# One decoder block on one core: residual loads per group, fills moved at the begin, and the last norm of self attention handed to cross attention's first batches

## Chip, cores, metric

One core of one Trainium2 chip. The metric is the device time of one execution in microseconds; the program is one launch. The matrices are f32; where a product needs more speed than f32 has, a value is kept as a high and a low part of type fp32r.

## The reference, cut

64 batches of 128 tokens with 128 features. All three parts end in a residual sum and a layer norm without weights.

```python
x = _layernorm(x + _L0_attn_ref(x, W_qkv, b_qkv, W_proj, b_proj))
x = _layernorm(x + _L0_xattn_ref(x, ctx_768, mask, Wq, Wk, Wv, Wo))
x = _layernorm(x + _L0_ffn_ref(x, phi_w, phi_b, expert_w, expert_b))
...
def _L0_attn_ref(...):
    attn = jnp.einsum('bsd,btd->bst', q, k) * SCALE
    attn = jax.nn.softmax(sps_pro(attn), axis=-1)   # x * mult, mult from four thresholds of sigmoid(x)
    return jnp.einsum('bst,btd->bsd', attn, v) @ W_proj + b_proj
def _L0_xattn_ref(...):                             # 16 heads of 8, 77 keys of 96 features
    scores = jnp.einsum('bhid,bhjd->bhij', q, k) * scale
    attn = jax.nn.softmax(jnp.where(mask, scores, -max), axis=-1)
    return jnp.einsum('bhij,bhjd->bhid', attn, v) @ Wo
```

The third part (soft mixture of 64 experts with 32 slots) is not touched by the change.

## The kernel before

The program is a row of blocks. In a block each engine has its own list, written out by hand; engines meet at semaphores (`wait_ge`; `reach` is the same but skips a wait for zero or less). A block ends when all five engines, SP with its DMA issues among them, have come to its end; only then does the next begin.

**`setup`** (L78 to L153). SP loads the weights and constants, ACT's queue the weights of cross attention. DVE spreads two biases (`brep`, L122), PE folds the weights of self attention (L145 to L153), DVE copies the results (L128 to L133). POOL fills partitions 96 to 127 of `w.xh` with ones (L138); `xh` and `xl` are the high and low part of the transposed x for the third part, whose row 127 is a constant row.

**`attention`** (L156 to L409). 16 groups of 4 batches; step k works on several groups at once. Group g passes through `groups(k, lag)`: products and scores at lag 0; thresholds (`band`, L352 to L357 on DVE, sums of them on POOL, L222 and L225), maxima and exponentials at lag 1; turning the weights and multiplying with the values at lag 2 (psum tile `O`); residual, statistics on DVE (L378 to L394) and the root on POOL (L228, L231) at lag 3; scaling on ACT (L309) and turning on PE (L296) at lag 4; the copy to `x1T` (L318) at lag 5. The steps run to GROUPS + 5. POOL first issues four loads of 1 MB of residuals into `xres`, fills `xl` (L214) and the two `pack` tiles (L217, L218). SP loads xT group by group (L237), two ahead. Near the end, steps 16 and 17 also make queries and keys of the first two pairs of batches for cross attention: PE L267 and L268, ACT's high part (L339), DVE's low part (L409). SP stores each pair to DRAM and loads it back in another layout:

```python
for r in FIRST:
    sync.wait_ge(w.low_ready, r + 1)
    store_and_pack(sync, w, r)
```

`store_and_pack` (L411) issues one store of the halves, waits for it, waits until the pack tile is free (`t_made`, counted in batches), and issues six loads into it.

**`attend_context`** (L428 on). Batch n = 0 to 63, pair r = n // 2. POOL multiplies packed keys (L822), PE makes scores in two halves (L567), DVE their maxima (L730), PE turns the maxima (L541) and makes turned scores and their shift (L579, L587, which raises `t_made`), ACT takes exponentials (L661), and one or more batches later PE, DVE and ACT do values, residual and norm. PE, ACT and DVE also make queries, keys (L528, L529) and values (L534) of later pairs. POOL clears two tiles (L813) and DVE three `vd` tiles in the first steps.

Of the kernel before, what the change touches and what calls it, by code (L numbers as in the profile page):

```python
# [18 lines left out]
ALU = mybir.AluOpType  # L19
ACT = mybir.ActivationFunctionType  # L20
X = mybir.AxisListType.X
F32 = mybir.dt.float32
# [55 lines left out]
def setup(nc, io, w):  # L78

    with ExitStack() as ctx:  # L80
# [54 lines left out]
        @block.gpsimd  # L135
        def _(pool):

            pool.memset(w.xh[96:128].bitcast(F32), 1.0)  # L138
# [16 lines left out]

def attention(nc, io, w):  # L156
# [3 lines left out]
    x_in = io["x"].rearrange("(q b s) d -> q s b d", q=4, s=S)  # L160
    with ExitStack() as ctx:
        st = Store(nc, ctx, "attn")
        xTg = [st.sb(f"xTg{i}", [128, GB * 128]) for i in range(2)]
# [9 lines left out]
        sums = [st.sb(f"sums{i}", [128, GB]) for i in range(2)]  # L173
        pT = [st.sb(f"pT{i}", [128, 512]) for i in range(2)]
        rinv = st.sb("rinv", [128, GB])
        y = [st.sb(f"y{i}", [128, GB, 128]) for i in range(2)]
        stats = st.sb("stats", [128, GB, 6])
        mv = [st.sb(f"mv{i}", [128, GB, 2]) for i in range(2)]
        veps = st.sb("veps", [128, GB])
        rstd = [st.sb(f"rstd{i}", [128, GB]) for i in range(2)]  # L180
        shift = [st.sb(f"shift{i}", [128, GB]) for i in range(2)]
        psU, psS, psT, psX = (st.ps(n, [128, 512]) for n in ("U", "S", "T", "X"))
        psO = [st.ps(f"O{i}", [128, 512]) for i in range(2)]
        psV = st.ps("V", [128, 2, 512])
        V = psV[:, :, 0:258].rearrange("p i (b e) -> p i b e", b=2)

        xT_loaded = [st.sem("xT_loaded0"), st.sem("xT_loaded1")]
        x_loaded = [st.sem(f"x_loaded{q}") for q in range(4)]
        (u_made, v_made, s_made, uT_ready, v_ready, rb_ready, a_ready, f_ready, p_ready, pT_made, pT_ready,
         o_made, mv_ready, rstd_ready, shift_ready, x1_ready, x1T_made, x1T_kept, low_ready, mult_ready, band_done, top_done,  # L190
         mx_done, y_chain, pool_chain) = (
            st.sem(n) for n in ("u_made", "v_made", "s_made", "uT_ready", "v_ready", "rb_ready", "a_ready",
                                "f_ready", "p_ready", "pT_made", "pT_ready", "o_made", "mv_ready",
                                "rstd_ready", "shift_ready", "x1_ready", "x1T_made", "x1T_kept", "low_ready",
                                "mult_ready", "band_done", "top_done", "mx_done", "y_chain", "pool_chain"))
        fill_made, row_set = st.sem("fill_made"), st.sem("row_set")
        WIDE = 256 + 2 * JP
        FIRST = range(2)
# [8 lines left out]
        STEPS = range(GROUPS + 5)  # L207

        @block.gpsimd
        def _(pool):  # L210
            for q in range(4):
                pool.dma_start(w.xres[:, q * 2048:(q + 1) * 2048].rearrange("s (b d) -> s b d", d=D), x_in[q])\
                    .then_inc(x_loaded[q], 16)
            pool.memset(w.xl[96:128].bitcast(F32), 0.0).then_inc(row_set, 1)  # L214
            pool.wait_ge(row_set, 1)
            for i in range(2):
                pool.tensor_copy(w.pack[i][:, :, 0:256], w.fill_row.unsqueeze(2).to_broadcast([128, 4, 256]))  # L217
                pool.memset(w.pack[i][:, :, 256:WIDE].bitcast(F32), 0.0).then_inc(w.pack_set, 1)  # L218
            for k in STEPS:
                for g in groups(k, 1):  # L220
                    pool.wait_ge(band_done, 2 * g + 2)
                    pool.tensor_tensor(band[4][:], band[1][:], band[2][:], ALU.add).then_inc(low_ready, 1)  # L222
                    pool.wait_ge(low_ready, g + 1)
                    reach(pool, f_ready, g)
                    pool.tensor_tensor(band[5][:], band[4][:], band[3][:], ALU.add).then_inc(mult_ready, 1)  # L225
                for g in groups(k, 3):
                    pool.wait_ge(mv_ready, g + 1)
                    pool.tensor_tensor(veps[:], mv[g % 2][:, :, 1], w.eps[:, 0:GB], ALU.add).then_inc(pool_chain, 1)  # L228
                    pool.wait_ge(pool_chain, g + 1)
                    reach(pool, x1_ready, g - 1)  # L230
                    pool.tensor_tensor(rstd[g % 2][:], veps[:], w.neg_half[:, 0:GB], ALU.pow).then_inc(rstd_ready, 1)  # L231

        @block.sync
        def _(sync):
            for g in range(GROUPS):
                reach(sync, s_made, g - 1)
                sync.dma_start(xTg[g % 2][:], io["xT"][:, residual(g)]).then_inc(xT_loaded[g % 2], 16)  # L237
                if g == 1:
                    sync.wait_ge(fill_made, 1)
                    sync.dma_start(w.fill_by_batch, w.fills[:]).then_inc(w.fill_stored, 16)  # L240
            for r in range(3):
                sync.dma_start(w.cg[r][:], io["ctxT"][:, r * 2 * JP:(r + 1) * 2 * JP]).then_inc(w.c_loaded[r], 16)
            sync.wait_ge(w.pack_set, 2)
# [6 lines left out]
        def _(pe):  # L250
            for k in STEPS:
# [10 lines left out]
                for r in [k - GROUPS] if k - GROUPS in FIRST else []:  # L262
                    pe.wait_ge(x1T_kept, 1)
                    pe.wait_ge(uT_ready, GROUPS)
                    reach(pe, w.low_ready, r)
                    pe.wait_ge(w.c_loaded[r], 16)
                    pe.matmul(psU[:, 0:256], w.xqs[:], w.x1T[:, r * 256:(r + 1) * 256], start=True, stop=True)  # L267
                    pe.matmul(psU[:, 256:WIDE], w.xk[:], w.cg[r][:], start=True, stop=True).then_inc(w.qk_made, 1)  # L268
                for g in groups(k, 2):
# [5 lines left out]
                    ins.then_inc(pT_made, 1)  # L275
                for g in groups(k, 0):
# [14 lines left out]
                for g in groups(k, 4):  # L291
                    pe.wait_ge(x1_ready, g + 1)
                    reach(pe, x1T_kept, g)
                    for b in range(GB):
                        c = slice(b * 128, (b + 1) * 128)
                        ins = pe.transpose(psX[:, c], w.xres[:, residual(g)][:, c], w.ident)  # L296
                    ins.then_inc(x1T_made, 1)

        @block.scalar
        def _(act):  # L300
            for k in STEPS:
# [4 lines left out]
                for g in groups(k, 4):  # L306
                    act.wait_ge(shift_ready, g + 1)
                    for b in range(GB):
                        ins = act.activation(w.xres[:, residual(g)][:, b * 128:(b + 1) * 128], y[g % 2][:, b, :],  # L309
                                             ACT.Identity, bias=shift[g % 2][:, b:b + 1], scale=rstd[g % 2][:, b:b + 1])  # L310
                    ins.then_inc(x1_ready, 1)
                for g in groups(k, 2):
                    act.wait_ge(pT_made, g + 1)
                    reach(act, o_made, g - 1)
                    act.copy(pT[g % 2][:], psT[:]).then_inc(pT_ready, 1)
                for g in groups(k, 5):
                    act.wait_ge(x1T_made, g + 1)
                    act.copy(w.x1T[:, residual(g)], psX[:]).then_inc(x1T_kept, 1)  # L318
                for g in groups(k, 0):
# [6 lines left out]
                    ins.then_inc(a_ready, 1)  # L326
                for g in groups(k, 1):
# [8 lines left out]
                for r in [k - GROUPS] if k - GROUPS in FIRST else []:  # L336
                    act.wait_ge(w.qk_made, r + 1)
                    reach(act, w.stored, 16 * r)
                    act.copy(w.qk[:, 0, :], psU[:, 0:WIDE]).then_inc(w.high_ready, 1)  # L339

        @block.vector
        def _(dve):
# [4 lines left out]
            for k in STEPS:  # L347
# [10 lines left out]
                for g in groups(k, 4):  # L358
                    dve.wait_ge(rstd_ready, g + 1)
                    reach(dve, x1_ready, g - 1)  # L360
                    dve.scalar_tensor_tensor(out=shift[g % 2][:], in0=mv[g % 2][:, :, 0], scalar=-1.0,
                                             in1=rstd[g % 2][:], op0=ALU.mult, op1=ALU.mult).then_inc(shift_ready, 1)
# [9 lines left out]
                for g in groups(k, 3):  # L372
                    if g == 0:
                        for q in range(4):
                            dve.wait_ge(x_loaded[q], 16)
                    dve.wait_ge(p_ready, g + 1)
                    reach(dve, mv_ready, g)
                    dve.reciprocal(rinv[:], sums[g % 2][:]).then_inc(y_chain, 1)  # L378
                    dve.wait_ge(o_made, g + 1)
                    dve.wait_ge(y_chain, 3 * g + 1)  # L380
                    reach(dve, x1_ready, g - 1)
                    for b in range(GB):
                        c = slice(b * 128, (b + 1) * 128)
                        ins = dve.scalar_tensor_tensor(out=y[g % 2][:, b, :], in0=psO[g % 2][:, c], scalar=rinv[:, b:b + 1],
# [1113 lines left out]
```

## Time and profile before

| | us |
|---|---|
| median of 3 runs | 1399.61 |
| all runs | 1399.61, 1403.23, 1399.18 |
| the profiled execution, its time | 1401.92 |
| its span | 1399.9 |

Busy over the span: PE 1293.0 us (92%), DVE 1109.3 (79%), ACT 896.6 (64%), POOL 1180.2 (84%). The mean granted TensorE clock is 0.975 of full speed. The profile was taken of one execution. Its rows have a start or a stretch in microseconds from the span's begin; "idle before" is time in which the engine did nothing before the row, with the event that ended it. An average over the span mixes stages with different limits, so the stretches around the change are read by themselves.

### The profile page before, as it was taken

How to read it: one execution, taken by the hardware profiler on the slowest of the kernel's cores; microseconds unless marked ns; L12 is line 12 of the kernel's file. 1: busy time of each engine (PE TensorE's matmuls, PEld its weight loads, DVE VectorE, ACT ScalarE, POOL GpSimd, SP SyncE). 2: the span in 40 equal slices, each digit the busy share in tenths (PEclk: the TensorE clock that was granted, in tenths of full speed). 3: DMA queues.
4: the chain of work that ended last, by engine and by line, in shares of the span. 5: the costliest groups of instructions: out<-in, count | busy, mean ns of one | idle time of the engine just before them, and what ended most of it. 6: DMA issues, size and time to landing. Idle time of an engine off the chain costs nothing. (4 is left out here: it accounts for less than half of the span.)

```text
span 1399.9 us, 31677 instructions
## 1 busy us (share of the span) xinstructions
PE 1293.0 (92%) x11006; PEld 1055.0 (75%) x11006; DVE 1109.3 (79%) x2462; ACT 896.6 (64%) x1670; POOL 1180.2 (84%) x1050
## 2 busy tenths in 40 slices
PE   4886789999999699999999999979999999999998
PEld 3664567777676477777777777748999999999997
DVE  4897456666666688888888888877999999999996
ACT  2897356666666476776776777735666666666664
POOL 7664568888888399999999999967999999999997
PEclk9998699999999999999999999999999999999999
DMA  5111243443443022222222222212222223232321
GB/s 167 47 40 55 84 134 117 121 122 115 125 121 94 24 84 89 92 83 91 91 84 90 91 87 87 84 48 94 84 88 83 88 84 89 82 91 80 92 79 31
DMA packets 83567, 123.61 MB, mean 88 GB/s; under 512 B 8593, under 2 KB 54226, under 8 KB 83410
## 3 DMA queue, kind: packets, MB, share of 16 engines
q1 hardware_dynamic: 81810, 117.16, 26.4%
q0 software_dynamic: 1088, 4.19, 1.0%
q8 instruction: 90, 1.47, 0.4%
q14 instruction: 67, 0.55, 0.1%
q10 hardware_dynamic: 512, 0.23, 0.1%
HBM read 70.28 MB, written 51.27 MB: 87 GB/s over the span
## 5 line engine op out<-in xcount | busy, mean ns | idle before, releaser
L997 POOL TENSOR_TENSOR gather_d<-gather_e,gather_rinv 128x1024 f32<-128x1024 f32 x128 | 244.8, 1913 | 36.6 <-DVE gather_rinv L976 36.5
L1256 POOL TENSOR_TENSOR mix_c<-mix_e,mix_rinv 128x1024 f32<-128x1024 f32 x128 | 240.9, 1902 | 18.7 <-DVE mix_rinv L1244 16.6
L1324 PEld LDWEIGHTS last_Y<-kept_phi,last_cT 128*128 128x128 f32 x2048 | 248.4, 192 | 7.3
L1324 PE MATMUL last_Y<-kept_phi,last_cT 128*128 128x128 f32 x2048 | 249.0, 275 | 0.0
L1340 ACT COPY last_cT<-last_T 128x1024 f32<-128x1024 f32 x128 | 128.4, 1003 | 132.1 <-PE last_T L1331 132.1
L822 POOL TENSOR_TENSOR cross_kd<-first_pack,kept_consts 128x624 fp32r<-128x624 f32 x128 | 155.6, 1237 | 63.7 <-DMA first_pack<-first_halves 54.1
L730 DVE TENSOR_REDUCE cross_mx<-cross_S 128x8 fp32r<-128x624 f32 x128 | 103.5, 809 | 113.0 <-PE cross_S L567 113.0
L1241 DVE TENSOR_REDUCE mix_sums<-mix_e 128x16 f32<-128x1024 f32 x128 | 155.8, 1217 | 34.4 <-ACT mix_e L1215 34.0
L972 DVE TENSOR_REDUCE gather_rsum<-gather_e 128x32 f32<-128x1024 f32 x128 | 156.1, 1220 | 25.9 <-ACT gather_e L945 25.9
L991 POOL TENSOR_TENSOR gather_dl<-gather_d,gather_dh 128x512 fp32r<-128x512 f32 x128 | 166.5, 1301 | 0.0
L934 ACT COPY gather_keep<-gather_L 128x256 f32<-128x256 f32 x256 | 94.7, 370 | 96.2 <-PE gather_L L908 95.9
L1331 PE MATMUL last_T<-kept_consts,mix_c 128*128 128x128 f32 x1024 | 134.2, 274 | 3.2 <-POOL mix_c L1256 1.1
L945 ACT ACTIVATE gather_e<-gather_L 128x1024 f32<-128x1024 f32 x128 | 131.1, 1024 | 7.5
L661 ACT ACTIVATE cross_pT<-cross_P 77x1024 f32<-77x1024 f32 x128 | 131.2, 1028 | 2.1 <-PE cross_P L587 2.1
L922 PE MATMUL slots_X<-gather_d,kept_xres 128*128 128x512 f32 x256 | 130.7, 592 | 0.0
L1249 POOL TENSOR_TENSOR mix_less<-mix_read,mix_high 128x1024 f32<-128x1024 f32 x64 | 122.5, 1914 | 7.4 <-DVE mix_high L1231 4.3
L1331 PEld LDWEIGHTS last_T<-kept_consts,mix_c 128*128 128x128 f32 x1024 | 114.6, 142 | 4.5 <-issue 2.5
L966 DVE TENSOR_REDUCE gather_mx<-gather_L 128x16 fp32r<-128x512 f32 x128 | 88.5, 691 | 30.3 <-PE gather_L L908 21.4
L927 PE MATMUL slots_X<-gather_dh,gather_x2h 128*128 128x512 f32 x128 | 101.0, 789 | 3.0 <-POOL gather_dl L991 3.0
L957 ACT CAST gather_dh<-gather_d 128x512 fp32r<-128x512 f32 x128 | 79.5, 621 | 31.6 <-PE slots_X L929 19.7
L968 DVE TENSOR_REDUCE gather_mx<-gather_L 128x16 fp32r<-128x512 f32 x128 | 87.0, 680 | 0.0
L908 PE MATMUL gather_L<-over_w1h,kept_xh 128*128 128x512 f32 x256 | 81.5, 400 | 4.3 <-ACT gather_e L945 3.3
(205 smaller groups left out, 3013.0 us busy)
## 6 DMA issues: line engine op xcount, KB each, us to landing
kept_logits<-gather_keep SPq DMA_DIRECT2D x128, 256.0 KB, 2.0
mix_read<-kept_logits SPq DMA_DIRECT2D x64, 512.0 KB, 3.7
first_halves<-first_qk SPq DMA_DIRECT2D x32, 412.0 KB, 3.0
first_pack<-first_halves SPq DMA_DIRECT2D x64, 128.0 KB
first_pack<-first_halves SPq DMA_DIRECT2D x32, 206.0 KB
first_pack<-first_halves SPq DMA_DIRECT2D x64, 78.0 KB
attn_xTg<-in_xT SPq DMA_DIRECT2D x16, 256.0 KB, 2.6
kept_xres<-in_x POOLq DMA_DIRECT2D x4, 1024.0 KB, 12.1
```

What stands on the lines that cost most here:

```text
L661: act.activation(pT[n % 2][0:J, hs, :, :], psP[:, hs, :, :], ACT.Exp)\
L822: pool.tensor_tensor(kd[n % 2][:, q], keys[:, q].to_broadcast([128, 2, 4, JP]), w.own.unsqueeze(1).unsqueeze(3).to_broadcast([128, 2, 4, J ...
L922: pe.matmul(psX[:, 2 * j + 1, :], w.xres[:, rows(u)], dd[u % 4][:, 1, :], start=first, stop=last)\
L945: act.activation(e[u % 2][:], psL[u % 2][:].rearrange("p i (n s) -> p i n s", n=16), ACT.Exp)\
L972: dve.tensor_reduce(rsum[u % 2][:].rearrange("p (i n) -> p i n", i=2), e[u % 2][:], X, ALU.add)\
L991: pool.tensor_tensor(dl[u % 2][:], dd[u % 4][:, 0, :], dh[u % 2][:], ALU.subtract).then_inc(dl_ready, 1)
L997: pool.tensor_tensor(dd[u % 4][:].rearrange("p i (n s) -> p i n s", n=16), e[u % 2][:], rinv[u % 2][:].rearrange("p (i n) -> p i n", i=2). ...
L1241: dve.tensor_reduce(self.sums[u % 2][:], self.e[u % 2][:], X, ALU.add).then_inc(self.sum_done, 1)
L1256: pool.tensor_tensor(self.cc[u % 2][:], self.e[u % 2][:], self.rinv[u % 2][:].unsqueeze(2).to_broadcast([128, 16, EXPERTS]), ALU.mult)\
L1324: ins = pe.matmul(psY[t % 2][:, 0:128], cT[u % 2][:, c, :], w.yk[:, 8 * (u % 2) + c, :], start=(u % 2 == 0 and c == 0), stop=(u % 2 == 1 a ...
L1331: ins = pe.transpose(psT[:, c, :], mix.cc[u % 2][:, 2 * c:2 * c + 2, :], w.ident)
L1340: act.copy(cT[u % 2][:], psT[:]).then_inc(cT_ready, 1)
```

## The change

- `setup`: SP also loads xT of groups 0 and 1, into tiles that now live outside `attention`. POOL's fill of `xh` goes; POOL fills the two pack tiles there, after `brep` (`rep` 3).
- `attention`: SP loads the residuals of each group behind that group's xT, 256 KB each; DVE waits for its group's. The constant rows of `xh` and `xl` come from a DRAM input by DMA, one partition each. The fills of `xl` and of the pack tiles and POOL's loads go. The steps run to GROUPS + 3. Pair 0's high part on ACT stands ahead of the last exponentials (L421 in the new order below), pair 1's queries and keys behind the last turning of weights.
- The norm of self attention becomes a class, `FirstNorm`, whose parts both blocks call. Group 14 is scaled and turned in cross attention, group 15 also summed, with statistics, root and shift there. They are turned in the psum tile `O` of cross attention, which lies on the bank of `O` of group 15.
- `attend_context`: SP begins with pair 1's store and packing. PE makes the first half of batch 0's scores first, then turns group 14, makes pair 2's queries and keys, and own values of pair 0 after the turned scores. The constant tile `pick`, which was made first, comes after batch 0's maxima.

```diff
@@ setup
+            for g in range(2):
+                sync.dma_start(w.xTg[g][:], io["xT"][:, g * 512:(g + 1) * 512]).then_inc(w.xT_loaded[g], 16)
             sync.dma_start(w.mask[:], io["mask"]).then_inc(w.mask_loaded, 16)
...
-            pool.memset(w.xh[96:128].bitcast(F32), 1.0)
+            pool.wait_ge(rep, 3)
+            for i in range(2):
+                pool.tensor_copy(w.pack[i][:, :, 0:256], w.fill_row.unsqueeze(2).to_broadcast([128, 4, 256]))
+                pool.memset(w.pack[i][:, :, 256:256 + 2 * JP].bitcast(F32), 0.0)
@@ attention
-        STEPS = range(GROUPS + 5)
+        def but_last(k, lag, left):
+            return [k - lag] if 0 <= k - lag < GROUPS - left else []
+        STEPS = range(GROUPS + 3)
...
-            for q in range(4):
-                pool.dma_start(w.xres[:, q * 2048:(q + 1) * 2048].rearrange("s (b d) -> s b d", d=D), x_in[q])\
-                    .then_inc(x_loaded[q], 16)
-            pool.memset(w.xl[96:128].bitcast(F32), 0.0).then_inc(row_set, 1)
...
-                reach(sync, s_made, g - 1)
-                sync.dma_start(xTg[g % 2][:], io["xT"][:, residual(g)]).then_inc(xT_loaded[g % 2], 16)
+                if g >= 2:
+                    sync.wait_ge(s_made, g - 1)
+                    sync.dma_start(xTg[g % 2][:], io["xT"][:, residual(g)]).then_inc(xT_loaded[g % 2], 16)
+                reach(sync, x_loaded[g % 4], 16 * (g // 4))
+                sync.dma_start(w.xres[:, residual(g)].rearrange("s (b d) -> s b d", d=D), x_in[g])\
+                    .then_inc(x_loaded[g % 4], 16)
...
+                if g == 3:
+                    sync.wait_ge(row_set, 16)
+                    sync.dma_start(w.xh[127:128].bitcast(F32), w.rows[0:1]).then_inc(row_set, 16)
+                    sync.dma_start(w.xl[127:128].bitcast(F32), w.rows[1:2]).then_inc(row_set, 16)
...
-            for r in FIRST:
-                sync.wait_ge(w.low_ready, r + 1)
-                store_and_pack(sync, w, r)
+            sync.wait_ge(w.low_ready, 1)
+            store_and_pack(sync, w, 0)
...
+                for g in but_last(k, 3, 1):
+                    dve.wait_ge(x_loaded[g % 4], 16 * (g // 4 + 1))
+                    norm.add_residual(dve, g, psO[g % 2])
@@ attend_context, SP
+            sync.wait_ge(low_ready, 2)
+            store_and_pack(sync, w, 1)
@@ attend_context, PE
                 if is_batch(n):
                     scores(n, 0)
+                if n == 0:
+                    pe.wait_ge(norm.y_chain, 3 * LAST + 2)
+                    norm.turn(pe, LAST - 1, all_O)
+                    queries_keys(2)
+                if n == 2:
+                    pe.wait_ge(norm.x1T_kept, LAST + 1)
...
+                if n == 1:
+                    norm.turn(pe, LAST, all_O)
@@ attend_context, ACT
+            norm.normalise(act, LAST - 1)
             for n in STEPS:
...
+                if n == 0:
+                    norm.keep_turned(act, LAST - 1, all_O)
...
+                if n == 0:
+                    keep_values(0)
+                    norm.normalise(act, LAST)
+                if n == 1:
+                    norm.keep_turned(act, LAST, all_O)
@@ attend_context, DVE
+            norm.add_residual(dve, LAST, w.last_O)
+            clear_values(0)
...
+                if n == 0:
+                    dve.tensor_copy(pick[:], w.sel.unsqueeze(2).to_broadcast([128, 4, JP])).then_inc(pick_set, 1)
+                    norm.find_shift(dve, LAST)
+                    clear_values(1)
@@ attend_context, POOL, between the keys of batch 0 and 1
+                if n == -1:
+                    norm.invert_spread(pool, LAST)
+                    pool.wait_ge(norm.rstd_ready, LAST + 1)
```

`FirstNorm`'s parts are the statements of before (L378 to L394, L228 to L231, L361, L309, L296, L318) with the group as argument.

How the rows move: SP's queue at the seam between the two attentions. Before, from the last context loads to the first load of cross attention (`first_halves` is the DRAM copy, `first_pack` the packed tile):

```order
L242 DMA first_cg<-in_ctxT 96x156 x3
L415 DMA first_halves<-first_qk 128x2x412
L420 DMA first_pack<-kept_fill 4x4x156
L424 DMA first_pack<-first_halves 32x1648
...
L415 DMA first_halves<-first_qk 128x2x412
L420 DMA first_pack<-kept_fill 4x4x156
L424 DMA first_pack<-first_halves 32x1648
...
L161 UNCONDITIONAL_BRANCH
L500 UNCONDITIONAL_BRANCH
L505 DMA first_cg<-in_ctxT 96x156
```

And now:

```order
L323 DMA first_cg<-in_ctxT 96x156 x3
L480 DMA first_halves<-first_qk 128x2x412
L485 DMA first_pack<-kept_fill 4x4x156
L489 DMA first_pack<-first_halves 32x1648
...
L248 UNCONDITIONAL_BRANCH
L568 UNCONDITIONAL_BRANCH
L480 DMA first_halves<-first_qk 128x2x412
L485 DMA first_pack<-kept_fill 4x4x156
L489 DMA first_pack<-first_halves 32x1648
...
L573 DMA first_cg<-in_ctxT 96x156
```

The block's end (the branches) stands before pair 1's store now, and the load of context 3 behind pair 1's packing.

PE at the same seam, from the last values of self attention. Before (`attn_X` are turned groups, `cross_M` queries, keys or values, `cross_S` scores, `cross_P` turned scores and shift):

```order
L289 MATMUL attn_O1<-attn_vp0,attn_pT1 128x128 x4
L296 MATMUL attn_X<-kept_consts,kept_xres 128x128 x12
L161 UNCONDITIONAL_BRANCH
L516 UNCONDITIONAL_BRANCH
L534 MATMUL cross_M<-first_xv,first_cg0 77x128 x2
L528 MATMUL cross_M<-first_x1T,first_xqs 128x256
L529 MATMUL cross_M<-first_cg2,first_xk 128x156
L567 MATMUL cross_S<-cross_kd0,first_pack0 128x312 x4
L541 MATMUL cross_M<-kept_neg_ident,cross_mx0 128x128
L579 MATMUL cross_P<-first_pack0 77x128 x16
L587 MATMUL cross_P<-cross_mT,cross_pick 77x128 x16
```

Now:

```order
L374 MATMUL attn_O1<-attn_vp0,attn_pT1 128x128 x4
L235 MATMUL attn_X<-kept_consts,kept_xres 128x128 x4
L248 UNCONDITIONAL_BRANCH
L586 UNCONDITIONAL_BRANCH
L637 MATMUL cross_S<-cross_kd0,first_pack0 128x312 x2
L235 MATMUL cross_O<-kept_consts,kept_xres 128x128 x4
L598 MATMUL cross_M<-first_x1T,first_xqs 128x256
L599 MATMUL cross_M<-first_cg2,first_xk 128x156
L637 MATMUL cross_S<-cross_kd0,first_pack0 128x312 x2
L611 MATMUL cross_M<-kept_neg_ident,cross_mx0 128x128
L649 MATMUL cross_P<-first_pack0 77x128 x16
L604 MATMUL cross_M<-first_xv,first_cg0 77x128 x2
```

Two turns of four have left the old block; the first scores stand first, one turn between their halves, and the own values of pair 0 behind the turned scores.

## Rows read from the trace of the kernel before

**Rows 1.** Windows: start:end, length, busy (count) by engine, PEclk, DMA share, GB/s

```profile
40.00:60.00 20.00, 15.65 (x110) 12.81 (x109) 18.67 (x94) 15.88 (x54) 13.40 (x13) 1.00 0.14 40
140.00:160.00 20.00, 11.56 (x91) 8.89 (x92) 7.42 (x14) 4.70 (x8) 13.39 (x10) 0.50 0.18 56
240.00:250.00 10.00, 9.36 (x160) 7.02 (x160) 6.59 (x21) 6.59 (x15) 8.41 (x11) 1.00 0.39 117
```

The busy columns are PE, PEld, DVE, ACT and POOL.

**Rows 2.** Order of time, POOL, the begin: start, duration, engine, line, what

```profile
0.72 6.92 POOL L138 MEMSET kept_xh<- 32x8192 f32 x1 [0.29 <-POOLq L1488]
...
18.13 6.95 POOL L214 MEMSET kept_xl<- 32x8192 f32 x1
...
28.99 1.26 POOL L222 TENSOR_TENSOR attn_band<-attn_band 128x512 f32<-128x512 f32 x1
```

**Rows 3.** Order of time, DVE, the begin

```profile
5.13 2.66 DVE L122 TENSOR_SCALAR setup_brep<-setup_ones,setup_bqkv 128x128 f32<-128x128 f32 x2 [4.10 <-DMA kept_consts<-in_consts]
...
21.05 4.32 DVE L352 TENSOR_SCALAR attn_band<-attn_a 128x512 f32<-128x512 f32 x1 [1.31 <-ACT attn_a L325]
...
32.68 0.43 DVE L352 TENSOR_SCALAR attn_band<-attn_a 128x512 f32<-128x512 f32 x1
...
38.16 0.43 DVE L352 TENSOR_SCALAR attn_band<-attn_a 128x512 f32<-128x512 f32 x1
```

**Rows 4.** Order of time, PE, the begin

```profile
7.94 0.77 PE L145 MATMUL setup_pa<-setup_wT 128*128 128x128 f32 x2 [7.94 <-DVE setup_brep L122]
...
15.36 2.08 PE L255 MATMUL attn_U<-attn_xTg,first_m 128*128 128x512 f32 x2 [3.80 <-DMA attn_xTg<-in_xT]
```

**Rows 5.** Order of time, SP's queue, the begin

```profile
12.76 0.81 SPq L237 DMA_DIRECT2D attn_xTg<-in_xT  x2
```

**Rows 6.** Order of time, SP's queue, the seam

```profile
126.80 0.39 SPq L415 DMA_DIRECT2D first_halves<-first_qk  x1
129.47 0.61 SPq L420 DMA_DIRECT2D first_pack<-kept_fill  x1
130.13 3.19 SPq L424 DMA_DIRECT2D first_pack<-first_halves  x5
133.37 0.59 SPq L415 DMA_DIRECT2D first_halves<-first_qk  x1
138.41 0.55 SPq L420 DMA_DIRECT2D first_pack<-kept_fill  x1
138.99 3.06 SPq L424 DMA_DIRECT2D first_pack<-first_halves  x5
```

**Rows 7.** Order of time, ACT and POOL, the seam

```profile
124.05 0.40 ACT L333 ACTIVATE attn_pr<-attn_f,attn_nb 128x128 f32<-128x128 f32 x1 [1.21 <-DVE attn_nb L406]
...
125.61 0.48 ACT L339 CAST first_qk<-attn_U 128x412 fp32r<-128x412 f32 x1
...
142.73 2.50 POOL L822 TENSOR_TENSOR cross_kd<-first_pack,kept_consts 128x624 fp32r<-128x624 f32 x2 [7.31 <-POOLq L161]
```

**Rows 8.** Order of time, all engines: the last group's norm

```profile
131.61 1.13 DVE L384 SCALAR_TENSOR_TENSOR attn_y<-attn_O,attn_rinv,kept_xres 128x128 f32<-128x128 f32 x4 [0.50 <-PE attn_O L289]
...
134.42 1.01 POOL L231 TENSOR_TENSOR attn_rstd<-attn_veps,kept_neg_half 128x4 f32<-128x4 f32 x1
...
135.66 1.65 ACT L309 ACTIVATE kept_xres<-attn_y,attn_shift,attn_rstd 128x128 f32<-128x128 f32 x4 [2.48 <-DVE attn_shift L361]
```

**Rows 9.** Order of time, PE: one turn, and the shift of batch 1

```profile
131.37 1.06 PE L296 MATMUL attn_X<-kept_consts,kept_xres 128*128 128x128 f32 x4
...
157.80 0.73 PE L587 MATMUL cross_P<-cross_mT,cross_pick 32*77 32x128 f32 x16
```

**Rows 10.** Order of time, ACT and PE, batches 6 to 8

```profile
183.44 0.50 ACT L683 CAST first_qk<-cross_M 128x412 fp32r<-128x412 f32 x1 [3.02 <-DMA first_halves<-first_qk]
...
186.37 0.76 PE L587 MATMUL cross_P<-cross_mT,cross_pick 32*77 32x128 f32 x16
...
193.30 0.47 PE L587 MATMUL cross_P<-cross_mT,cross_pick 32*77 32x128 f32 x16
...
198.22 0.47 PE L587 MATMUL cross_P<-cross_mT,cross_pick 32*77 32x128 f32 x16
```

More of the change, by code:

```diff
@@ L225, in _ @@
                     pool.tensor_tensor(band[5][:], band[4][:], band[3][:], ALU.add).then_inc(mult_ready, 1)
[L226 to L231, printed above, removed]
+                for g in but_last(k, 3, 1):
+                    norm.invert_spread(pool, g)
         @block.sync
@@ L261, in _ @@
                     ins.then_inc(v_made, 1)
[L262 to L268, printed above, removed]
+                if k == GROUPS:
+                    queries_keys(0)
                 for g in groups(k, 2):
@@ L290, in _, with keep_weights, high_part @@
                     ins.then_inc(o_made, 1)
[L291 to L297, printed above, removed]
+                for g in but_last(k, 4, 2):
+                    norm.turn(pe, g, psX)
         @block.scalar
         def _(act):
+            def keep_weights(k):
+                for g in groups(k, 2):
+                    act.wait_ge(pT_made, g + 1)
+                    reach(act, o_made, g - 1)
+                    act.copy(pT[g % 2][:], psT[:]).then_inc(pT_ready, 1)
+            def high_part(r):
+                act.wait_ge(w.qk_made, r + 1)
+                reach(act, w.stored, 16 * r)
+                act.copy(w.qk[:, 0, :], psU[:, 0:WIDE]).then_inc(w.high_ready, 1)
             for k in STEPS:
@@ L305, in _ @@
                     act.activation(uT[:], psU[:], ACT.Identity, bias=w.cvec[:]).then_inc(uT_ready, 1)
[L306 to L318, printed above, removed]
+                if k >= GROUPS:
+                    keep_weights(k)
+                for g in but_last(k, 4, 2):
+                    norm.normalise(act, g)
+                if k < GROUPS:
+                    keep_weights(k)
+                for g in but_last(k, 5, 2):
+                    norm.keep_turned(act, g, psX[:])
                 for g in groups(k, 0):
@@ L335, in _ @@
                     ins.then_inc(p_ready, 1)
[L336 to L339, printed above, removed]
+                if k == GROUPS + 1:
+                    high_part(1)
         @block.vector
@@ L357, in _ @@
                     dve.tensor_scalar(band[2][:], av, T_01, -0.4, ALU.is_lt, ALU.mult).then_inc(band_done, 1)
[L358 to L362, printed above, removed]
+                for g in but_last(k, 4, 1):
+                    norm.find_shift(dve, g)
+                if k == STEPS[-1]:
+                    for q in range(4):
+                        dve.wait_ge(x_loaded[q], 64)
                 for g in groups(k, 0):
@@ L371, in _ @@
                        .then_inc(v_ready, 1)
[L372 to L384, printed above, removed]
[L385 to L395 removed]
+                for g in but_last(k, 3, 1):
+                    dve.wait_ge(x_loaded[g % 4], 16 * (g // 4 + 1))
+                    norm.add_residual(dve, g, psO[g % 2])
                 for g in groups(k, 1):
@@ L1437, in decoder_block @@
             w.halves = nc.dram_tensor("first_halves", (2, 2, 128, wide), F32, kind="Internal").ap()
-            w.qk_made, w.high_ready, w.low_ready, w.stored, w.pack_set, w.t_made = (
-                sf.sem(n) for n in ("qk_made", "high_ready", "low_ready", "stored", "pack_set", "t_made"))
+            w.qk_made, w.high_ready, w.low_ready, w.stored, w.t_made = (
+                sf.sem(n) for n in ("qk_made", "high_ready", "low_ready", "stored", "t_made"))
             w.packed = [sf.sem("packed0"), sf.sem("packed1")]
-            setup(nc, io, w)
-            attention(nc, io, w)
+            w.norm = FirstNorm(sf, w)
+            with ExitStack() as early:
+                w.xTg = [early.enter_context(nc.sbuf_tensor(f"first_xTg{i}", [128, 512], F32)) for i in range(2)]
+                setup(nc, io, w)
+                attention(nc, io, w)
             x1T_space.close()
@@ L1485 @@
         "expert_w": get("L0_ffn_expert_w"), "expert_bT": get("L0_ffn_expert_b").T,
-        "consts": constants(),
+        "consts": constants(), "rows": np.stack([np.ones(TOKENS, np.float32), np.zeros(TOKENS, np.float32)]),
     }
```

182 lines of the change are left out of this document (127 added, 55 removed).

## Prediction

> **What bounds the kernel now.** I read the windows by stage first, to find which engine is full where; then the order of time on POOL, DVE and PE over the first 45 us; then the order of time around the seam between the two attentions, on SP's queue above all. Everything behind the first batches of cross attention is left alone by the change.
>
> In self attention DVE is the full engine: 18.67 of 20 us from 40 to 60 [rows 1], and one group of four batches costs DVE some 6 us. In cross attention PE is full: 9.36 of 10 us in a late window [rows 1]. From 140 to 160 nobody is: PE 11.56, DVE 7.42 of 20 us, with PE's granted clock at 0.50, the 1.2 GHz level [rows 1]. So there are two places with time to give, the begin and the seam, and each is a chain of waits, not a sum of work.
>
> The begin. POOL fills a quarter of `xh` until 7.64 (0.72 + 6.92) and a quarter of `xl` until 25.08 (18.13 + 6.95) [rows 2]. Two small DVE instructions behind the first fill show 2.66 us and end at 7.79; one DVE comparison that takes 0.43 elsewhere shows 4.32 and ends at 25.37, right behind the second fill [rows 2, 3]. PE starts its folding at 7.94, 0.15 us after the first of these ends, is done at 11.56 (15.36 less 3.80), and waits those 3.80 for a load of xT that SP issued at 12.76, with the start of the block [rows 4, 5]. POOL reaches its first addition of `band` at 28.99 [rows 2], so the first comparison of the second group comes 11.63 us after that of the first (21.05 to 32.68); the next follows in 5.48 [rows 3].
>
> The seam. SP stores pair 0's halves at 126.80, waits 2.67, issues six packing loads in 3.85, stores pair 1 at 133.37, waits 5.04 and issues six more, until 142.05 (138.99 + 3.06) [rows 6]. Only then does the block end: POOL's first key product starts at 142.73, released by the block's branch and not by its data [rows 7].
>
> **The change, part by part.** Sums are against the profiled execution: 1401.92 us, a span of 1399.9. The median of the runs is 1399.61, 2.3 below, and I take the same gain off it.
>
> 1. *No fill of xh.* DVE's two products start at 5.13; alone they are an estimate of 0.1 to 0.2 us each (0.43 for four times the columns [rows 3]), so they end at 5.5 instead of 7.79. The PE folding hangs on them directly: **-2.3**. Cost of what moves in: the two pack fills, 3.9 us in all on POOL (25.08 to 28.99 [rows 2]), run from 5.5 to 9.4 now. PE's folding ends at 9.2 (11.56 less 2.3), DVE's copies come behind it, and the block starts at 10.5 (12.76 less 2.3), so POOL is covered. If DVE's three small instructions in between wait for all of POOL's, DVE reaches its copies at 10.0 rather than 9.25: the bounds are 0 and +0.8. I take 0, since the copies wait for PE anyway.
> By the Trainium skill (SBUF — State Buffer, "Who interferes with whom") whichever of DVE in a two-port mode and GpSimd issues first holds the shared ports for its whole instruction, and the other fully blocks. The 4.32 us agree; by that rule the moved fills speak against this part, and the sum would be 0.8 us higher.
>
> 2. *xT loaded in setup.* Issued at 3.0 and landed long before 10. PE's first matmul starts with the block, 12.8 less 2.3, rather than at 15.36: **-2.6**. The two loads now stand ahead of the mask and behind the constants on SP; they can delay the constants, released at 5.13, by between nothing and about half a microsecond. I take nothing.
>
> 3. *No fill of xl, no pack fills and no four 1 MB loads at the head of POOL's list.* The first group's comparison takes 0.43, POOL adds right away, and the distance to the second group's becomes the 5.48 of the next pair in place of 11.63 [rows 3]: **-6.15**. The third xT load, in flight beside 4 MB of residuals before, is no longer late. What takes their place: one residual load of 256 KB per group on SP's queue, two issues per group instead of one where SP waits for PE most of the time. Each is issued two groups ahead of the DVE step that reads it, more than 12 us. Two rows of 32 KB go to one partition each; no row shows such a load, but nothing waits for them until the first packing, 100 us later. Cost nothing; one more DVE wait per group, fifteen times under 0.1 us.
>
> Begin: 2.3 + 2.6 + 6.15 = **-11.0**, and self attention, full on DVE, carries it to the seam unchanged.
>
> 4. *Pair 0's high part ahead of the last exponentials.* Times here are those of the trace before, without the 11.0. The exponentials take ACT from 124.05 to 125.61 [rows 7]; the copy now comes before them, where ACT had waited 1.21 for DVE, at about 123.8. DVE is done with the last maxima at 124.0 and makes the low part at once. The store moves from 126.80 to 125.0: **-1.8**. Its price, some 0.3 us of later exponentials, lies beside the store.
>
> 5. *Pair 1's store and packing behind the block's end, the last two groups' turn and the last group's norm too.* SP: store at 125.0, landed 127.7 (2.67), packing issued by 131.5 (3.85) [rows 6]. DVE and ACT end at about 130.9 by the same walk, two groups' chains shorter. So the block ends at 131.5 and the next begins at 132.2 (0.68 as before, 142.05 to 142.73). Now data bind: pair 0's packing lands later than the branch. No row shows when a packing lands. From both sides: a lone store of the same halves took 2.28 from the end of its issue (127.19 to 129.47), the store behind a packing 5.04 from its start [rows 6]; the least is the block's own 0.68. I take 2.3, since nothing stands ahead of this packing: the first key product comes at 133.8 instead of 142.73, **-8.9** with the 1.8 of point 4 in it; the bounds make it 10.5 to 6.2.
>
> 6. *What comes into the first batches.* One norm is a chain of 5.7 us, from DVE's first sum at 131.61 over POOL's root (134.42, 1.01) to the end of ACT's scaling at 137.31 [rows 8]. DVE's part of it, 2.8 us (131.61 to 134.42), comes ahead of its first maximum, from 132.3 to 135.1 with one clearing behind it, at 136; the first scores are not there before 135.9 (first half of the keys 1.25 after 133.8, then 0.9 of PE). POOL's root stands between the keys of batch 0 and 1 and is done before PE asks for the latter. PE has two turns more, 1.06 each at the low level [rows 9]; the first fills PE's wait for the first maximum, and the own values of pair 0 move behind it. Walking each queue: PE's shift of batch 1, which frees the pack for pair 2, ends 16.0 us after the first key product, and 15.8 before (142.73 to 158.53 [rows 7, 9]). Cost **+0.2**; bounds 0 and +3.0. Pair 1's packing: store at 132.3, 5.04, 3.85 of issues, 2.3 of landing, 143.5, about when POOL first asks for it and 6 us before PE needs its keys. Behind batch 1 the queues stand in the old order, and PE-bound cross attention carries the gain on.
>
> Sum: -11.0 - 8.9 + 0.2 = -19.7. Profiled 1382.2; **1379.9 us** on the median, a gain of 1.4%. A measurement of this kernel can tell about 0.3%, 4.2 us, from no change.
>
> **The rivals.**
> *The moved work lies on the path again (0.12).* The last norm's chain (5.7 us) and two turns (2.1 us) stand before batch 1's shift and come one behind another: 7.8 of the 8.9 go back, **1387.7**. For it: every engine has it early in its list, and in-order queues pass a wait on. Against it: PE was idle for 8.4 of 20 us in exactly that stretch [rows 1].
> *The old stall goes (0.07).* ACT waited 3.02 for a store of the halves, until 183.44, and the batch after took 6.93 (PE's shifts at 186.37 and 193.30) instead of 4.92 (to 198.22) [rows 10]. If the new spacing of SP's work misses it, 5 us more are gained: **1374.9**. Against it: that piece of SP's list is unchanged and hangs on PE's shifts.
> *The begin does not do what it says (0.04).* The pack fills were moved, not removed, and the early loads share the rings with the constants; point 1 and 2 lose most of their 4.9: **1384**.
> *Slower: PE stays at 1.2 GHz (0.04).* The seam's low stretch ends only when PE has become busy again. The new first batches have more short waits between PE's pieces. A batch at the low level costs 6.93 against 4.92 [rows 10], 2.0 more; the gain of 19.7 is gone after 10 batches more at that level, and "slower" is reached from 12. With 16, **1412**. For it: 0.50 held over all of 140 to 160 [rows 1]. Against it: with the same batch order PE got out of it before, while idle more than it will be. The Trainium skill (TensorE: Matmul & The Clock Gate, "The HAM clock gate") says that throttled is the default and activity releases it, which would favour this rival where idle gaps grow; here they shrink.
>
> **How the numbers follow.** The forecast has 0.73. Its own bounds (0.8, 0.5, 2.7 and 1.6 of landing, 3.0) give 1378 to 1387. To hold 8 in 10 I reach to the stall's case below and the path's case above: 1373 to 1389. Faster: all but the last rival, 0.96; half of that rival's 0.04 ends within 0.3%, half above: same 0.02, slower 0.02.
>
> **What would show it.** PE's folding starting near 5.6 and the first self attention matmul near 10.5 with no DMA wait; the comparisons of groups 0 and 1 5.5 apart, at 16.2 and 21.7; a DVE-full stretch with no wait for `in_x`; the first key product near 122.8 and released by DMA; PE's second shift ending near 138.8. Wrong would be: a first comparison of 4 us in spite of the missing fill, DVE waits for residual loads, PE at 1.2 GHz beyond 145, or a first maximum of batch 0 that starts on DVE's account and not PE's.

## The result, and the profile after

Median 1380.79 us (1379.94 to 1382.79, 4 runs) against 1399.39 (1397.85 to 1403.23, 4 runs) for the kernel before: a ratio of 0.9865, 95% interval 0.9846 to 0.9884, so 18.6 us less, between 16 and 22. The profiled execution took 1381.27 us, with a span of 1379.2.

The begin, in order of time, DVE and POOL of the changed kernel (start, duration, engine, line, what, idle time before and its releaser). They answer to [rows 2, 3].

```profile
5.67 0.48 DVE L124 TENSOR_SCALAR setup_brep<-setup_ones,setup_bqkv 128x128 f32<-128x128 f32 x2 [4.64 <-DMA kept_consts<-in_consts]
6.07 0.22 DVE L125 CAST kept_ident<-kept_consts 128x128 f16<-128x128 f32 x1
6.21 0.22 DVE L126 TENSOR_SCALAR kept_neg_ident<-kept_consts 128x128 fp32r<-128x128 f32 x1
6.34 1.06 DVE L128 TENSOR_SCALAR first_xqs<-first_xq 128x128 f32<-128x128 f32 x1
9.96 0.29 DVE L130 COPY first_m<-setup_pa 128x128 f32<-128x128 f32 x1 [2.56 <-PE setup_pb L158]
...
16.98 0.43 DVE L438 TENSOR_SCALAR attn_band<-attn_a 128x512 f32<-128x512 f32 x1 [1.31 <-ACT attn_a L411]
...
22.47 0.43 DVE L438 TENSOR_SCALAR attn_band<-attn_a 128x512 f32<-128x512 f32 x1
```

```profile
6.22 1.10 POOL L142 CAST first_pack<-kept_consts 128x1024 fp32r<-128x1024 f32 x1 [5.80 <-DVE setup_brep L124]
...
8.88 0.61 POOL L143 MEMSET first_pack<- 128x624 f32 x1
18.77 1.27 POOL L298 TENSOR_TENSOR attn_band<-attn_band 128x512 f32<-128x512 f32 x1 [9.27 <-DVE attn_band L443]
```

The two products take 0.48 and not 2.66, the first comparison 0.43 and not 4.32, and the second comes 5.49 behind the first and not 11.63. POOL is done with the pack fills at 9.49, before DVE's copies at 9.96, and then waits 9.27 for DVE. PE, to compare with [rows 4]:

```profile
6.30 0.77 PE L150 MATMUL setup_pa<-setup_wT 128*128 128x128 f32 x2 [6.30 <-DVE setup_brep L124]
...
11.16 2.04 PE L343 MATMUL attn_U<-first_xTg,first_m 128*128 128x512 f32 x2 [1.24 <-PEq L80]
```

The wait of 3.80 for xT is now one of 1.24 for the block's start. The seam on SP's queue and POOL, against [rows 6, 7]:

```profile
114.32 0.38 SPq L480 DMA_DIRECT2D first_halves<-first_qk  x1
117.31 0.62 SPq L485 DMA_DIRECT2D first_pack<-kept_fill  x1
117.98 3.08 SPq L489 DMA_DIRECT2D first_pack<-first_halves  x5
121.71 0.39 SPq L480 DMA_DIRECT2D first_halves<-first_qk  x1
124.58 0.57 SPq L485 DMA_DIRECT2D first_pack<-kept_fill  x1
125.19 3.06 SPq L489 DMA_DIRECT2D first_pack<-first_halves  x5
```

```profile
123.41 2.43 POOL L920 TENSOR_TENSOR cross_kd<-first_pack,kept_consts 128x624 fp32r<-128x624 f32 x2 [5.08 <-DMA first_pack<-first_halves]
```

The block ends behind pair 0's packing (121.06), and the first key product waits for data, no longer for the branch: it starts 2.35 after the last issue. PE's shift of batch 1, against [rows 9]:

```profile
132.00 0.78 PE L657 MATMUL cross_P<-cross_mT,cross_pick 32*77 32x128 f32 x16
138.10 0.73 PE L657 MATMUL cross_P<-cross_mT,cross_pick 32*77 32x128 f32 x16
```

It ends at 138.83, 15.42 after the first key product. One of the prediction's signs of being wrong stands on its edge: the first maximum of batch 0 shows no wait for PE. PE's first scores ended at 125.65 and DVE's clearing at 125.68:

```profile
124.79 0.86 PE L637 MATMUL cross_S<-cross_kd,first_pack 128*128 128x312 f32 x2 [5.34 <-POOL cross_kd L920]
125.59 0.09 DVE L808 MEMSET cross_vd<- 128x32 f32 x1
125.76 0.81 DVE L819 TENSOR_REDUCE cross_mx<-cross_S 128x8 fp32r<-128x624 f32 x1
```

In the trace with the early xT loads behind the constants (an experiment below) the scores ended at 125.23 and the maximum started at 125.57, so there it was on DVE's account, by some 0.3 us. And the old stall is still there, against [rows 10]:

```profile
164.24 0.50 ACT L771 CAST first_qk<-cross_M 128x412 fp32r<-128x412 f32 x1 [4.01 <-DMA first_halves<-first_qk]
```

The same points in the kernels before and after and in those of the first two experiments, read from the order of time in each:

| us from the span's begin | constants release DVE | second comparison | first key product | shift of batch 1 ends | wait of ACT at pair 5 | median time |
|---|---|---|---|---|---|---|
| before | 5.13 | 32.68 | 142.73 | 158.53 | 3.02 | 1399.39 |
| changed | 5.67 | 22.47 | 123.41 | 138.83 | 4.01 | 1380.79 |
| begin alone | 5.09 | 22.36 | 130.17 | 145.97 | 4.07 | 1388.99 |
| seam alone | 5.08 | 32.68 | 136.13 | 150.61 | 2.36 | 1390.85 |
| begin, store moved | 5.41 | 22.76 | 129.63 | 145.43 | 4.11 | 1388.30 |
| begin, norm moved | 5.00 | 22.73 | 129.52 | 145.13 | 4.08 | 1387.44 |

### The profile page after: what moved, and what is told of

The parts are those of the page before. It is cut to its first block and busy times, and to the rows that moved or that the text cites. A ratio compares the mean times of both kernels' runs of the same rounds, so it can differ in the third digit from the quotient of the medians.

```text
span 1379.2 us, 31693 instructions
## 1 busy us (share of the span) xinstructions
PE 1286.2 (93%) x11006; PEld 1050.8 (76%) x11006; DVE 1105.5 (80%) x2462; ACT 896.5 (65%) x1670; POOL 1162.0 (84%) x1044
## 5 line engine op out<-in xcount | busy, mean ns | idle before, releaser
L1067 DVE TENSOR_REDUCE gather_mx<-gather_L 128x16 fp32r<-128x512 f32 x128 | 88.6, 692 | 29.6 <-PE gather_L L1009 20.7
```

## The experiments

### Do the two parts add?

`begin alone` is the kernel before with the change's setup, loads and rows; the seam is left as it was.

```diff
+            for g in range(2):                       # setup, as in the change
+                sync.dma_start(w.xTg[g][:], io["xT"][:, g * 512:(g + 1) * 512]).then_inc(w.xT_loaded[g], 16)
...
             for r in FIRST:                          # attention, as before
                 sync.wait_ge(w.low_ready, r + 1)
                 store_and_pack(sync, w, r)
```

> The begin of the change alone (early xT, residual loads per group, constant rows by DMA, pack fills in setup); the seam is that of before. Theory A (two chains that add): the comparison of the last group comes about 10.3 us earlier (near 108.1, as in the changed kernel), the first key product near 132.4 (142.73 less 10.3), time near 1389. Theory B (the begin's gain is swallowed by a later wait or given back by the 16 more loads): the last comparison near 110 or later, time above 1393.

Measured: 1388.99 us (4 runs) beside 1398.20 (7 runs) of the kernel before, ratio 0.9926 (0.9908 to 0.9945). The last group's comparison stands at 107.99, 10.45 earlier. The first key product, though, is at 130.17, 12.6 earlier and not 10.3. The reason is in its SP queue, against the fourth and fifth of [rows 6]:

```profile
122.76 0.59 SPq L418 DMA_DIRECT2D first_halves<-first_qk  x1
125.84 0.56 SPq L423 DMA_DIRECT2D first_pack<-kept_fill  x1
```

Pair 1's store waits 3.08 here, 5.04 in the profile of the kernel before. The last experiment below, which has the old begin and the old seam, shows 3.05 and its key product at 140.75. From the last group's comparison to the first key product the profile of before has 24.29, `begin alone` 22.18 and that last experiment 22.21. So some 2 us of the old seam look like that one profiled execution's own, which was also 2.5 above the median; no second trace of the kernel before itself was taken.

`seam alone` is the changed kernel with the old setup, fills and four 1 MB loads:

```diff
-            pool.wait_ge(rep, 3)
-            for i in range(2):
-                pool.tensor_copy(w.pack[i]...)
+            pool.memset(w.xh[96:128].bitcast(F32), 1.0)
...
+            for q in range(4):
+                pool.dma_start(w.xres[:, q * 2048:(q + 1) * 2048]..., x_in[q]).then_inc(x_loaded[q], 16)
+            pool.memset(w.xl[96:128].bitcast(F32), 0.0).then_inc(row_set, 1)
```

> The seam of the change alone; setup, POOL's fills and its four 1 MB loads are those of before. Theory A (the two parts add): first comparison at 21.05 and 32.68 as before, first key product near 133.7 (142.73 less 9.0), shift of batch 1 ending near 149, time near 1390. Theory B (the seam depends on what the begin freed): key product later than 136, time above 1394.

Measured: 1390.85 us (4 runs), ratio 0.9941 (0.9921 to 0.9962). The second comparison is at 32.68, but the last group's at 121.12, 2.7 later than in the kernel before: DVE waited once for PE inside self attention, at 55.45, where the granted clock is 0.50 from 50 to 55 (0.83 over 40 to 60). Why it fell there was not tested.

```profile
DVE attn_rb L443 <- PE attn_V L341: 2.7, 1, 2.7
```

(Waits of DVE from 44 to 112: who waited for whom, us, times, longest.) From the last comparison to the key product it takes 15.01, in the changed kernel 15.32, with the begin alone 22.18. So the seam is worth 6.9 (22.18 less 15.32) with the new begin and 7.2 (22.21, from the last experiment, less 15.01) with the old, and theory A holds, with this size in place of 9.0. Its key product at 136.13 lies just past the 136 of theory B; the 2.7 are what carried it there. Saved by the begin 9.2, by the seam 7.4, by both 18.6, each with 2 to 3 us of uncertainty: they add within it.

### What of the seam carries it?

Once only the store and packing of pair 1 move, once only the norms. The first diff is to `begin alone`, the second to the changed kernel.

```diff
-            for r in FIRST:
-                sync.wait_ge(w.low_ready, r + 1)
-                store_and_pack(sync, w, r)
+            sync.wait_ge(w.low_ready, 1)
+            store_and_pack(sync, w, 0)
@@ attend_context
+            sync.wait_ge(low_ready, 2)
+            store_and_pack(sync, w, 1)
```

> The begin of the change, and of the seam only pair 1's store and packing moved behind the block's end; the last groups' norms stay in self attention. Theory A (SP and the norm chain end within 3 us of each other, so that both must move): the block ends with ACT's last copy, 139.62 less 10.3, key product near 130, time near 1386.6, only 2.4 below the begin alone. Theory B (SP's list alone held the block): key product near 125.2, time near 1382.

```diff
-            sync.wait_ge(w.low_ready, 1)
-            store_and_pack(sync, w, 0)
+            for r in range(2):
+                sync.wait_ge(w.low_ready, r + 1)
+                store_and_pack(sync, w, r)
@@ attend_context
-            sync.wait_ge(low_ready, 2)
-            store_and_pack(sync, w, 1)
```

> The changed kernel with pair 1's store and packing back in the self attention block. Theory A: SP stores pair 1 at 121.1, packs from 124 to 126 until 128 to 130, block end behind it, key product between 128.5 and 130.5, time near 1387. Theory B (the norm chain alone held the block): key product near 123.4, time near 1381.

Measured: 1388.30 and 1387.44 us (2 runs each), ratios 0.9924 (0.9901 to 0.9948) and 0.9918 (0.9890 to 0.9947). The first key product of each, in this order:

```profile
129.63 2.51 POOL L826 TENSOR_TENSOR cross_kd<-first_pack,kept_consts 128x624 fp32r<-128x624 f32 x2 [4.50 <-POOLq L166]
```

```profile
129.52 2.43 POOL L919 TENSOR_TENSOR cross_kd<-first_pack,kept_consts 128x624 fp32r<-128x624 f32 x2 [10.34 <-POOLq L248]
```

Both wait for the block's end, as before. Against the begin alone (130.17) each half gains under 1 us; with both moved it is 6.8. Counted from the last group's comparison it is 1.0, 1.6 and 6.9. What held the block is the norm chain's last copy on ACT in the first, until 129.34, and SP's packing in the second, until 128.85:

```profile
128.75 0.59 ACT L322 COPY first_x1T<-attn_X 128x512 f32<-128x512 f32 x1 [1.27 <-PE attn_X L300]
```

```profile
125.78 3.07 SPq L490 DMA_DIRECT2D first_pack<-first_halves  x5
```

SP's list and the norm chain ended side by side, and the block waits for the later. Theory A, in both runs.

### What of the begin carries the 6.15?

The fill of `xl` alone back on POOL, and the four big loads alone back:

```diff
+            pool.memset(w.xl[96:128].bitcast(F32), 0.0).then_inc(pool_set, 1)
+            pool.wait_ge(pool_set, 1)
```

> The changed kernel with the fill of xl (partitions 96 to 127) back at the head of POOL's list in self attention, and nothing else before it. Theory A (the fill costs only what of it reaches beyond the first comparison): fill 11.5 to 18.5, first comparison shows about 2 us and ends near 18.7, second comparison 1.5 later than 22.47, time +1.5. Theory B (the fill by itself carried the 6.15 of the prediction's third point): second comparison near 28.6, time +6.

```diff
-                sync.dma_start(w.xres[:, residual(g)]..., x_in[g]).then_inc(x_loaded[g % 4], 16)
+            for q in range(4):
+                pool.dma_start(w.xres[:, q * 2048:(q + 1) * 2048]..., x_in[q]).then_inc(x_loaded[q], 16)
```

> The changed kernel with POOL's four 1 MB residual loads in place of the loads per group, no fills. Theory A (4 MB in flight delay the third xT load, which is in nobody's way only while POOL is late anyway): first matmul of group 2 near 24 instead of 18.87, third comparison about 3 us later than 28.21, time +3. Theory B (the loads cost nothing without the fills): third comparison within 0.5 us of 28.21, time the same.

With the fill: 1381.53 us (2 runs), second comparison at 24.28, 1.8 later. Not the comparison was blocked, but a mask instruction of 64 x 77 ahead of it, and DVE's queue behind that:

```profile
10.51 6.92 POOL L296 MEMSET kept_xl<- 32x8192 f32 x1 [1.63 <-POOLq L80]
...
10.59 6.90 DVE L436 TENSOR_SCALAR first_fills<-first_mask 64x77 f32<-64x77 uint8 x1
...
14.36 3.13 DVE L456 TENSOR_SCALAR attn_rb<-attn_V,first_beta 128x4 f32<-128x4 f32 x1
...
17.55 1.14 ACT L415 ACTIVATE attn_a<-attn_S,attn_rb 128x128 f32<-128x128 f32 x4 [4.22 <-DVE attn_rb L456]
...
18.72 0.43 DVE L442 TENSOR_SCALAR attn_band<-attn_a 128x512 f32<-128x512 f32 x1 [1.23 <-ACT attn_a L415]
```

With the big loads: 1382.23 us (2 runs, 1379.44 and 1385.03), second comparison at 22.13, third at 30.73 where the changed kernel has 28.21. PE's third group waits for its xT:

```profile
24.22 2.08 PE L343 MATMUL attn_U<-first_xTg,first_m 128*128 128x512 f32 x2 [5.81 <-DMA first_xTg<-in_xT]
```

Theory A in both, though with the fill the first comparison was late for another reason than it gave: neither alone carries the 6.15. In the kernel before, the second comparison stood behind DVE's maxima of the first group, and these waited for POOL, whose list of issues, fill and pack fills ran until 28.99:

```profile
31.62 0.29 DVE L401 CUSTOM_DVE_ANT_0 attn_f<-attn_band,attn_a 128x128 f32<-128x128 f32 x1 [3.42 <-POOL attn_band L225]
```

That the whole list together makes the 6.15 is read from this trace; the pack fills were not put back by themselves. The times of two runs each don't tell 1 us; the points in the traces do.

### Do the early loads delay the constants?

```diff
+            sync.wait_ge(loaded, 16 * len(loads))
             for g in range(2):
                 sync.dma_start(w.xTg[g][:], ...
```

> The changed kernel, with SP waiting for the constants before it issues the early xT loads. Theory A (the early loads delayed the constants by the 0.54 us that their release moved, 5.13 to 5.67): DVE's first product at 5.1, PE's folding at 5.8 instead of 6.30, first matmul of self attention near 10.65 instead of 11.16, time 0.5 lower, which only the trace can tell. Theory B (the constants are late for another reason): 5.67 stays.

DVE was released at 5.09 and the first matmul stood at 10.57, as theory A has it. But so it was in kernels that keep the early loads: 5.09, 5.41 and 5.00 in the table, and 5.06 to 5.24 in five more. So the 5.67 looks like one execution's landing, and theory A is not borne out, with one trace of each kernel. Time 1378.42 us (2 runs), no difference that can be told. In that trace the second comparison is at 22.55, no earlier than the changed kernel's 22.47: see the last section.

### The stall

The 5 us rival named a stall that the change left in place. The load of phi (1 MB) and its bias were issued between pair 3's packing and pair 4's store. Moved into self attention:

```diff
+                if g == 8:
+                    sync.dma_start(w.phi[:], io["phi"].rearrange("(c r) d -> r c d", r=128)).then_inc(w.phi_loaded, 16)
+                    sync.dma_start(w.bias[:], io["phi_b"]).then_inc(w.phi_loaded, 16)
@@ attend_context
-                if r == 4:
-                    sync.dma_start(w.phi[:], ...
-                    sync.dma_start(w.bias[:], ...
```

> The changed kernel, with the loads of phi (1 MB) and its bias issued in self attention, behind group 8's xT, instead of between two pairs in cross attention. Theory A (these two issues and 1 MB on SP's queue make the store of pair 4 late, ACT waits 4.01 us for it and PE's clock falls): no wait over 1.5 us at that place, batches 5 to 7 some 4.9 apart instead of 8.99 and 6.55, time 5 to 6 us below the changed kernel, near 1375. Theory B (the stall is of the store's own queue): the wait stays at 3 us or more, time 1380 to 1382.

> The changed kernel with only the bias of phi (8 KB in rows of 64 bytes, an issue of 2.03 us) loaded early; phi itself (1 MB) stays between pairs 3 and 4. Theory A (it is the megabyte in front of the store): the wait of ACT at pair 5 stays at 2 to 3 us, time 1378 to 1380. Theory B (it is the bias's issue and its many small pieces): the wait goes, time near 1375.

> The changed kernel with only phi (1 MB) loaded early; the bias stays between pairs 3 and 4. Theory A (the megabyte): wait below 1 us, time near 1375 to 1376. Theory B (the bias): wait of 3 us or more, time near 1380.

> The kernel before the change with both loads of phi issued behind group 8's xT. Theory A (the stall is there without the change too and is worth its 3.0 us wait and the 2.0 us of one batch at the low clock): time 4 to 6 us below the kernel before. Theory B (the stall matters only where the change put it, since its wait is 4.0 there): less than 3 us.

Both early: **1374.91 us** (5 runs, 1374.04 to 1374.96), ratio to the kernel before 0.9831 (0.9817 to 0.9846). ACT waits no more for a store there, and PE's shifts of batches 5 to 7 come 4.9 and 4.7 apart, not 9.0 and 6.6. First the changed kernel, then this one:

```profile
158.28 0.47 PE L657 MATMUL cross_P<-cross_mT,cross_pick 32*77 32x128 f32 x16
167.27 0.73 PE L657 MATMUL cross_P<-cross_mT,cross_pick 32*77 32x128 f32 x16
173.82 0.47 PE L657 MATMUL cross_P<-cross_mT,cross_pick 32*77 32x128 f32 x16
```

```profile
157.94 0.47 PE L657 MATMUL cross_P<-cross_mT,cross_pick 32*77 32x128 f32 x16
162.86 0.47 PE L657 MATMUL cross_P<-cross_mT,cross_pick 32*77 32x128 f32 x16
167.52 0.47 PE L657 MATMUL cross_P<-cross_mT,cross_pick 32*77 32x128 f32 x16
```

Windows of the same two (PE, PEld, DVE, ACT, POOL, clock, DMA, GB/s):

```profile
160.00:170.00 10.00, 5.88 (x87) 4.85 (x91) 3.62 (x11) 3.90 (x10) 4.77 (x7) 0.74 0.57 163
```

```profile
160.00:170.00 10.00, 9.41 (x185) 7.22 (x174) 6.61 (x21) 6.82 (x16) 9.63 (x13) 1.00 0.41 119
```

Only the bias early: 1380.36 us (4 runs, ratio 0.9862, 0.9848 to 0.9877), ACT waits 3.60. Only phi early: 1374.63 us (4 runs, ratio 0.9825, 0.9809 to 0.9842), no wait. It is the megabyte: these two, measured side by side, lie 5.7 apart. In the kernel before, both loads early gave 1396.17 us (7 runs) beside 1399.72 (10 runs), ratio 0.9969 (0.9957 to 0.9981): 4.3 less by the ratio, 3.6 by the medians, at the low end of theory A, and the interval reaches into B's. Its runs lie in two clusters, near 1393 and 1397; why, stays open. The kernels with phi early on the changed begin and seam are the fastest of this study.

## Why the prediction was right

The forecast was 1379.9, measured 1380.79. By its steps:

1. *No fill of xh, -2.3*: the folding began 1.64 earlier (7.94 to 6.30), since the constants came 0.54 later in this execution; 1.9 to 2.3 in the nine experiments with this begin (5.63 to 6.03). The cover held: of three small DVE instructions one waited for POOL's copy (1.06 where 0.22 is usual), and the copies waited for PE all the same. The 0.8 us that I worked out beside the Trainium skill's rule (SBUF — State Buffer, "Who interferes with whom") were not paid: the lock agrees with the 1.06, which ended at 7.40 behind POOL's copy (7.32), but the other two (6.07 and 6.21) started before that copy (6.22).
2. *xT in setup, -2.6*: from folding to first matmul 7.42 before, 4.86 now, -2.56.
3. *-6.15*: 11.63 to 5.49, -6.14. Between the first matmul and the first comparison I kept 5.69; it took 5.82 here and 6.1 to 6.8 in eight experiments. The comparisons stood at 16.98 and 22.47, not 16.2 and 21.7. That is the begin's miss, in the profiled execution for the late constants, in the eight for this stretch: -10.35 at the last group (118.44 to 108.09), not -11.0.
4. *-1.8*: from the last comparison to the store 8.36 before, 6.23 now, -2.1.
5. *-8.9*: against the profile -19.32 less 10.35, so -8.97, with the packing landing after 2.35 where I took 2.3. But the 5.04 of [rows 6] was in it as if it were the kernel's; two kernels with the same list there show 3.05 and 3.08, and the seam is worth 6.9 to 7.2. So this term was some 2 us too large. The profiled 1401.92 was 2.5 above the median, and I took the same gain off the median.
6. *+0.2*: 15.80 to 15.42, -0.4. The norm in the first batches cost nothing, its rival falls. In six of the seven experiments that have both moves of the seam the same distance is 14.4 to 14.5, and each has a window of 5 us at a granted clock of 0.70 to 0.84 on the way; in the changed kernel and in the one with the fill back (15.42 too) it is 0.50 in every window from 125 to 140. One batch later all eight agree within 0.5 (batch 2's shift ends 20.9 to 21.3 after the first key product), and the profile of before has 22.1: by then the gain is some 1 us. Why the clock differs was not tested.

Behind batch 1 the gain of 19.7 was carried on: 20.2 at batch 5, 19.5 behind the stall, 20.7 at the span's end. The begin's 10.4, the seam's 6.9 and batch 0 and 1's 0.4 make 17.7 of the 18.6 between the medians (18.2 with batch 2's shift as the end); the rest is within the interval. So the mechanism was right, and that the number came within 0.9 us is in part luck: the seam's gain was put some 2 us and the begin's 0.7 us too high, and the first batches came out 0.6 us or more better than put. The stall stayed (4.01, 3.02 before), PE did not stay at the low level, and the rival that had the kernel slower was never near: the clock was at 0.92 again from 140 to 145.

## What to carry to other kernels

Where a block ends with its slowest engine, list every engine's last instruction before moving anything: two lists that end side by side give little one at a time (0.5 and 0.7 us at the first key product here) and 6.8 together. Keep a bulk load away from a queue whose next store somebody waits for: 1 MB moved to a stretch that is full on DVE gave 5.7 to 5.9 us, a third of what the whole change had. And before a wait of one profiled execution enters a sum, ask for it in a second trace.

## What the runs showed of the hardware

- A fill of 6.92 us on POOL held up a DVE instruction on 64 x 77 elements for 6.90 us, and two that read PSUM behind it in the queue; the cost then showed at ACT, not at DVE.
- PE starting 0.3 to 0.7 us earlier at the begin gained 0.3 us at most in eight traces (first comparison at 16.65 to 17.27, in the changed kernel 16.98). First matmul at 11.16 in the changed kernel and at 10.49 in `begin, norm moved`, first comparison at 16.98 and 17.24. The granted clock is listed as 1.00 there, but durations are those of the 1.2 GHz level (2.05 for two matmuls that take 1.02 later), and the third step still was in the latter kernel:

```profile
10.49 2.05 PE L344 MATMUL attn_U<-first_xTg,first_m 128*128 128x512 f32 x2 [1.24 <-PEq L80]
...
14.05 1.91 PE L367 MATMUL attn_S<-first_xTg,attn_uT 128*128 128x128 f32 x8
```

where the changed kernel has 1.06. Why the level rose at the same time in both was not tested.
- The store of the halves took 2.6 to 3.4 us at the seam, in the profile of before once 5.04. With the megabyte in front of it on the queue it took 5.8 in the changed kernel and 5.2 to 7.8 in the others that have it there.
